# A second cross-attention whose maxima products move from zero-padded query tiles to row groups of the array

## The reference

```python
q = qkv.reshape(bs * N_HEADS, ch, length)
k = v = y.reshape(bs * N_HEADS, ch, -1)
scale = 1.0 / math.sqrt(math.sqrt(ch))
weight = jnp.einsum('bct,bcs->bts', q * scale, k * scale)
weight = jax.nn.softmax(weight.astype(jnp.float32), axis=-1).astype(weight.dtype)
a = jnp.einsum('bts,bcs->bct', weight, v)
```

## Time and profile before

| | us |
|---|---|
| median of 3 executions | 1993.25 |
| lowest, highest | 1988.57, 2001.61 |
| the profiled execution, its device time | 1990.66 |
| the profiled execution, its span | 1988.8 |

### The profile page before, as it was taken

The page is one execution under the profiler, slowest core; times in us unless marked ns, Lnnn a source line. Parts: engine busy times, 40 slices in busy tenths (PEclk is TensorE's granted clock), DMA queues, the critical chain, the costliest instruction groups (busy, mean ns, idle before and its releaser), DMA issues. The chain is left out here.

```text
span 1988.8 us, 23904 instructions
## 1 busy us (share of the span) xinstructions
PE 1719.1 (86%) x8103; PEld 871.0 (44%) x8134; DVE 1290.5 (65%) x1649; ACT 777.5 (39%) x1275; POOL 829.1 (42%) x369
## 2 busy tenths in 40 slices
PE   5999999994656777899999998999999986989996
PEld 2444444442444543444444444444444323444443
DVE  3668989857898775766666665666666413565553
ACT  1211212113444533565655555655565554011010
POOL 0012222012554426577776676777767660000000
PEclk9999999996788876999999998999999996999999
DMA  8030312302000045143344444443332302000002
GB/s 320 9 114 20 89 44 66 124 34 82 1 0 0 0 104 142 39 105 92 87 98 105 105 105 106 105 94 78 89 86 70 71 1 87 1 0 0 0 0 85
DMA packets 83551, 137.19 MB, mean 69 GB/s; under 512 B 16606, under 2 KB 53490, under 8 KB 82678
## 3 DMA queue, kind: packets, MB, share of 16 engines
q1 hardware_dynamic: 83446, 135.84, 25.0%
HBM read 70.73 MB, written 8.66 MB: 40 GB/s over the span
## 5 line engine op out<-in xcount | busy, mean ns | idle before, releaser
L1257 DVE TENSOR_REDUCE c_piece_max<-c_unit 128x1 f32<-128x804 f32 x512 | 484.2, 990 | 280.4 <-PE c_unit L1383 277.1
L1342 ACT ACTIVATE c_prob<-c_scores 128x512 f32<-128x512 f32 (+1 forms) x832 | 472.2, 596 | 365.6 <-PE c_scores L1400 356.4
L1192 POOL TENSOR_TENSOR c_prob_sum<-c_prob_sum,c_prob 128x2048 f32<-128x2048 f32 x96 | 439.7, 4580 | 68.3 <-ACT c_prob L1342 64.3
L1400 PE MATMUL c_scores<-c_queries,c_keys 98*128 98x512 f32 (+1 forms) x832 | 358.1, 451 | 30.9 <-ACT c_prob L1342 16.6
L1383 PE MATMUL c_unit<-c_khigh,c_qdiag 128*128 128x402 f32 x1024 | 315.0, 393 | 23.3 <-DVE c_piece_max L1257 12.5
L1383 PEld LDWEIGHTS c_unit<-c_khigh,c_qdiag 128*128 128x128 f32 x1024 | 189.0, 204 | 175.9 <-DVE c_piece_max L1257 92.3
L1409 PE MATMUL c_out<-c_prob,c_VT 128*32 128x512 f32 (+1 forms) x1664 | 228.4, 629 | 22.1 <-issue 22.1
L1400 PEld LDWEIGHTS c_scores<-c_queries,c_keys 98*128 98x128 f32 (+1 forms) x832 | 158.0, 193 | 186.6 <-ACT c_prob L1342 132.3
L525 PE MATMUL a_S<-a_ctxT,a_xnT 128*128 128x401 f32 x512 | 188.9, 513 | 7.2 <-ACT a_prob L490 3.9
L555 PE MATMUL a_o<-a_ctx,a_probT 128*128 128x512 f32 (+1 forms) x416 | 181.2, 592 | 0.0
L1192 POOL TENSOR_TENSOR c_prob_sum<-c_prob 128x2048 f32<-128x2048 f32 x16 | 72.5, 4534 | 137.0 <-ACT c_prob L1342 137.0
(11 more groups left out here) (204 smaller groups left out, 2099.1 us busy)
## 6 DMA issues: line engine op xcount, KB each, us to landing
c_keys<-c_khigh SPq DMA_DIRECT2D x128, 200.2 KB, 3.0
c_k<-in_keys SPq DMA_DIRECT2D x16, 801.0 KB, 6.3
c_keys<-c_k SPq DMA_DIRECT2D x64, 200.2 KB, 3.0
a_ctx<-in_ctx SPq DMA_DIRECT2D x12, 1024.0 KB, 5.4
c_VT<-in_values SPq DMA_DIRECT2D x16, 768.0 KB
a_ctxT<-in_ctxT SPq DMA_DIRECT2D x12, 802.0 KB, 4.8
c_queries<-c_qhigh SPq DMA_DIRECT2D x128, 64.0 KB, 2.6
a_weights<-in_L_ffn_weight SPq DMA_DIRECT2D x3, 1408.0 KB, 13.6
```

What stands on the lines that cost most here:

```text
L1192: nc.gpsimd.tensor_tensor(psum4[:], a[:], prob[(j * MC + c) % RING][:], ALU.add).then_inc(sums_taken, 2 if i == 1 else 1)
L1257: nc.vector.tensor_reduce(piece_max[j % 2][:, k // 2, k % 2:k % 2 + 1], U[bank(unit)][:, :, 0:PIECE], axis=AX.XY, op=ALU.max).then_inc(uni ...
L1342: nc.scalar.activation(prob[(j * MC + c) % RING][0:w, h, :], STp[h % 2][0:w, :], ACT.Exp, scale=SCALE).then_inc(exp_done, 1)
L1400: nc.tensor.matmul(STp[h % 2][0:w, :], K[p][:, h, c * P:c * P + w].bitcast(F32R), Q[p][:, h, :].bitcast(F32R), start=True, stop=True).then ...
```

## The change

The padded tiles go. A unit is now two heads, one block of queries and one piece of keys. Each of its two matmuls reads the head's own 32 partitions of `qhigh` (weights) and `khigh` (streamed), and is placed on those 32 rows of the array by `tile_position`: heads 0 and 1 on rows 0 to 31 and 32 to 63, heads 2 and 3 on the other two. The number of units, of matmuls, their columns, the banks and the place of each unit in the program stay. The reduction reads the same 2 x 402 values, but gives a maximum for each bank instead of one for both. The two memsets, the four DMAs of each group and the waits for them go; the first unit of a group waits for `qhigh` itself, and `qhigh` is written anew only when TensorE is through with the last unit that read it.

```diff
-        PAIRS = H * TB * 2
+        PIECES, PER = len(STARTS), 2
+        PAIRS = H // PER * TB * PIECES
...
-        QZ = [sb(f"c_qdiag{j}", [P, H, D]) for j in range(2)]
...
+        def part(k):
+
+            return k // (TB * PIECES) * PER, k // PIECES % TB, k % PIECES
...
             load_keys(0, 0)
             load_keys(1, 1)
-            sp.wait_ge(consts_ready, 3)
-            load_diagonal(0, 0)
-            sp.wait_ge(consts_ready, 4)
...
-                if more:
-                    load_diagonal(g + 2, j % 2)
...
-            steps.link(pool.memset(QZ[0][:], 0.0))
             rest_of_q(0, 0)
             rest_of_k(0, 0)
-            steps.link(pool.memset(QZ[1][:], 0.0))
...
-                nc.vector.tensor_reduce(piece_max[j % 2][:, k // 2, k % 2:k % 2 + 1], U[bank(unit)][:, :, 0:PIECE], axis=AX.XY, op=ALU.max).then_inc(unit_read, 1)
+                h0, t, piece = part(k)
+                nc.vector.tensor_reduce(piece_max[j % 2][:, h0:h0 + PER, t, piece], U[bank(unit)][:, :, 0:PIECE], axis=AX.X, op=ALU.max).then_inc(unit_read, 1)
...
-                    act.wait_ge(diag_loaded, (n - 1) * DIAGS)
+                    act.wait_ge(unit_full, FULL0 + place(n - 2, PAIRS - 1) + 1)
...
-                h, t, half, o = k // (2 * TB), k // 2 % TB, k % 2, j % 2
+                (h0, t, piece), o = part(k), j % 2
                 if k == 0:
-                    pe.wait_ge(diag_loaded, (n + 1) * DIAGS)
+                    pe.wait_ge(qhigh_ready, n + 1)
                     pe.wait_ge(khigh_ready, n + 1)
                 pe.wait_ge(unit_read, place(n, k) + 1)
-                for e in range(2):
-                    at = STARTS[2 * half + e]
-                    last = nc.tensor.matmul(U[bank(unit)][:, e, 0:PIECE], QZ[o][:, h, t * P:(t + 1) * P].bitcast(F32R), khigh[o][:, at:at + PIECE], start=True, stop=True)
+                at = STARTS[piece]
+                for e in range(PER):
+                    head = slice((h0 + e) * CH, (h0 + e + 1) * CH)
+                    last = nc.tensor.matmul(U[bank(unit)][:, e, 0:PIECE], qhigh[o][head, t * P:(t + 1) * P], khigh[o][head, at:at + PIECE],
+                                            start=True, stop=True, tile_position=((h0 + e) * CH, 0))
                 last.then_inc(unit_full, 1)
```

More of the change, by code:

```diff
@@ L1003, in cross_attention_1 @@
         nhalf = sb("c_nhalf", [P, 1])
-        piece_max = [sb(f"c_piece_max{j}", [P, H * TB, 2]) for j in range(2)]
+        piece_max = [sb(f"c_piece_max{j}", [P, H, TB, PIECES]) for j in range(2)]
         nmax = sb("c_nmax", [P, H, TB])
@@ L1008, in cross_attention_1 @@
         rden = sb("c_rden", [P, D])
-        U = [ps(f"c_unit{j}", [P, 2, 512]) for j in range(2)]
+        U = [ps(f"c_unit{j}", [P, PER, 512]) for j in range(2)]
         STp = [ps(f"c_scores{h}", [P, D]) for h in range(2)]
@@ L1023, in cross_attention_1 @@
         stacked = sem("c_stacked")
-        diag_loaded = sem("c_diag_loaded")
         unit_full = sem("c_unit_full")
@@ L1042, in cross_attention_1 @@
         FINS = 1
-        STACKS, ROWS, DIAGS = 16 * H * 6, 16 * H, 16 * H
+        STACKS, ROWS = 16 * H * 6, 16 * H
         EXPS0, PV0, UNITS0, FULL0, SCORES0 = 2, RING, 2, 1, 1
@@ L1260, in maximum @@
                     dve.wait_ge(unit_read, UNITS0 + place(n, k) + 1)
-                    nc.vector.tensor_reduce(nmax[:].rearrange("p h t -> p (h t)"), piece_max[j % 2][:], axis=AX.X, op=ALU.max, negate=True).then_inc(nmax_ready, 1)
+                    nc.vector.tensor_reduce(nmax[:], piece_max[j % 2][:], axis=AX.X, op=ALU.max, negate=True).then_inc(nmax_ready, 1)
             def keep_rows(unit):
@@ L1436, in slot @@
                         rows(unit) if unit[0] == "rows" else pair(unit)
-                    pe.wait_ge(consts_ready, 7)
+                    pe.wait_ge(consts_ready, 5)
                     for h in range(H):
```

## The result

The change made the kernel slower: median 2080.89 us (2073.66 to 2089.57, 4 executions) against 1992.72 us, a ratio of 1.0438 with a 95% interval of 1.0384 to 1.0492. That is +88 us where +43 was forecast. The time lies inside the stated range and the sign is right, but the size is off by a factor of two.

A forecast was written before the change was run, and what follows sets the result against it. TensorE's pace was taken to bound each slot's body; 59 (units between scores) - 5 (behind outputs) - 9 (VectorE waits) - 2 (lead-in) = +43 us, forecast 2036 us, range 1972 to 2092.

The forecast's parts named there:

- Price of the switched unit: Unit between two scores in stage c: 0.78 us instead of 0.61, +0.17 each; 345 units, +59 us.
- The 4-row matmul of stage a: Model for a switch of array division: starts 0.09 us late, its load not ahead; next matmul 0.27 us later.
- Base that it was set against: Kernel before, unit between scores: 0.24 us from score to unit and 0.37 to the next score, 0.61 together.
- Units behind outputs: Units behind outputs or denominators, where a switch exists already: 0.44 us instead of 0.48; 119 units, -5 us.
- The waits for VectorE: 37 short TensorE waits in stage c for VectorE to free a unit bank would vanish: -9 us.
- The lead-in: Before the slots, without the second memset, SP's copies start at 726.5 instead of 728.27: -2 us.
- The clock: Granted TensorE clock in the slots: the sum gave it no term, leaving a lower clock to a rival.
- a rival with 0.12: Clock rival: each of 15 slots spends 7 us more at the low level, +45 us, 2081; chance 0.12.
- one stretch with scores and outputs alone: Sign against the clock rival: behind the last unit, TensorE busy 23.36 of 27 us, the clock stayed at 1.00.

The follow-up runs named there:

- the tiny matmul: Kernel before, plus one matmul of 32 rows and 2 columns at the head of each unit, adding switches and removing no pass: 2138.58 us, ratio 1.0728.
- The pair of slots above: One slot each of the changed kernel and the kernel before, both with 12 scores a slot issued twice: 2054.04 and 1991.41 us; the slots differ by 2.0 us.
- the one on four row groups: Changed kernel with units issued two at a time, their four matmuls on four row groups: 2148.12 us, ratio 1.0741.
- one pass: Kernel before with padded full-height tiles, each unit in the slots issuing only its first matmul: 1957.41 us, ratio 0.9823.
- Full-height repeats: Changed kernel with the 12 scores of the first three key chunks of each slot, from the second slot on, issued twice: 2054.04 us, ratio 1.0252.
- repeats on two row groups: Changed kernel with both matmuls of each unit issued twice, same values into the same place: 2199.5 us, ratio 1.1045.

## Why the prediction was right or wrong

**Price of the switched unit: right.** 0.78 us forecast, 0.80 seen in the tightest place; the tiny matmul, which only switches, gave 0.99 against 0.98. The 4-row matmul of stage a was a good model.

**Base that it was set against: a term mis-sized.** "Together 0.78 instead of 0.61" took 0.61 from the tightest place of a slot. The 313 units between scores that I can follow at full clock in the trace of before take 0.752 us on average from score to next score; the 294 after take 0.818. Before, about 114 of the 313 stand behind a score whose load was bare, and in about 96 the next score comes more than 0.40 us after the unit, as here:

```profile
1126.88 0.53 PE L1383 MATMUL c_unit<-c_khigh,c_qdiag 128*128 128x402 f32 x2
1127.50 0.50 PE L1400 MATMUL c_scores<-c_queries,c_keys 98*128 98x512 f32 x1
1127.83 0.53 PE L1383 MATMUL c_unit<-c_khigh,c_qdiag 128*128 128x402 f32 x2
1128.20 0.40 PE L1400 MATMUL c_scores<-c_queries,c_keys 98*128 98x512 f32 x1
```

Here (kernel before) the score at 1127.50 comes 0.62 us after its unit, not 0.37, because it waited for the exponential that freed its bank, which ended at 1127.44, and its load was bare, so the next unit follows after 0.33 and not 0.24. A switch falls into such gaps for nothing. So +0.066 us and not +0.17: 345 x 0.066 = 23 us instead of 59. The pair of slots above gives 2.0 us for a full set of 32 units, and 15 such sets make 30; so 23 to 30.

**Units behind outputs.** 0.04 less forecast, nothing gained or lost seen: 0.38 us to the score and a bare load of 0.11, 0.49 against 0.48. A miss of 5 us.

**The waits for VectorE.** As forecast: 37 waits, 9.5 us before; after, between 770 and 1670 us, one:

```profile
PE c_unit L1373 <- DVE c_piece_max L1246: 0.5, 1, 0.5
```

But this is part of the 0.752, and was counted beside it.

**The lead-in.** -1.8, as forecast.

**The clock: the step that failed.** The sum took the granted clock in the slots as unchanged, at nothing, and the prediction had it beside the sum as a rival with 0.12. The runs show that it is the largest term. The low level in the slots rose from 84 to 236 us; at the 0.38 us that each costs this is 58 of the 80.7 us, and the 23 that are left are the switches at their mean price. With 30 us for the switches it would be 51. That the rival's 2081 is the time that came is luck: it added 45 us for the clock to 43 for the rest, and the one was too small by about as much as the other was too large. By the slots: one of before with no low level in it is 52.6 us,

```profile
890.99:943.62 52.63, 49.22 (x273) 24.13 (x272) 35.66 (x41) 32.43 (x57) 39.05 (x14) 1.00 0.41 99
```

with 2.0 for switches an estimated 54.6; after the change none with a full set of units is without it, and they are 58.4 to 67.6 us. The prediction had named what spoke for the rival: the low level that already stood at each slot's start, the lead-in that stayed at 0.50 with one unit after another, and that half of the rows work while a unit streams. It let one stretch with scores and outputs alone outweigh them, in which no unit runs at all.

**Stage d.** 9.9 us of the 89 are in a stage that no edit touches. From the last reciprocal to the end its low level was 68 us against 47, which at 0.38 is 8 of them. In the profiled executions of all kernels this stretch took 350 to 360 us, the longer the more low level it had (47 us in the shortest, 68 in the longest), and without order by the edit: 360 in the kernel before with 12 repeated scores, 350 in the one on four row groups. So I hold its share for chance; why the clock fell more often there isn't shown.

**What is open.** What of a matmul the clock goes by. Two runs part the change in two. Half of the streaming gone and no switch (one pass) has 34 us more low level in the slots than before; switches added and no pass gone (the tiny matmul) has 94; the change, which does both, has 152. So here the added switches lengthened the low level by more than the halved streaming did. How far the two add up isn't shown, since single traces differ by tens of us; over the whole program, by the medians of all executions, the three numbers are 30, 104 and 157. Full-height repeats raised the clock (0.88 to 0.95); repeats on two row groups did not (0.85); all four row groups in one pass had the lowest but one (0.78). In these last ones pauses and rows in use change together. The division of the 51 to 58 us between slower matmuls and the waits that follow from them isn't shown either.

## What to carry to other kernels

A change that takes work from TensorE, or puts pauses between its matmuls, can lower its clock. Cost it twice, at the clock of before and with a longer stretch at 1.2 GHz, and read in the granted clock of each stage whether it already falls there. The price of that stretch can be had beforehand, from executions of the same kernel that differ in their clock (0.38 us for each us here). And take the base of a price from the mean over all places, not from the tightest one: where the engine already pauses, added latency is hidden and removed work returns less (0.11 us for a pass of 0.17 here). Zero padding that streams for free under a wait can be the cheaper form.

## What I had not expected of the hardware

- More work made the program faster, in both kernels: 180 matmuls more took 27 us off the changed kernel, and 120 more took 17 us off the one before (ratio 0.9913).
- TensorE's busy share rose from 86% to 88% of the span while its clock fell; the busy share in a profile doesn't tell what clock it will be granted.
- A two-column matmul on 32 rows between full-height ones costs 0.26 us on average (1.012 us from score to score against 0.752), nearly all of it in changing over.
- Adding such switches and taking no work away lowered the slots' clock from 0.95 to 0.91.
